# One-hots and spread positions of a graph layer built by two-tensor compares

## The reference

```python
x_j = x[src]
x_i = x[dst]
msg = concatenate([x_i, x_j - x_i], axis=-1)
h = relu(msg @ W1 + b1)
h = relu(h @ W2 + b2)
h = relu(h @ W3 + b3)
m = h @ W4 + b4
s = segment_sum(m, dst, 12500)
cnt = segment_sum(ones, dst, 12500)
out = layernorm(x + s / maximum(cnt, 1)[:, None])
```

## Time and profile before

| | us |
|---|---|
| median of 3 runs | 1553.71 (1542.68 to 1553.79) |
| the profiled execution | 1556.37 |
| its span, first to last instruction | 1554.5 |
| busy: matrix engine, weight loads | 1375.3, 930.6 |
| busy: Vector engine, ScalarE, GpSimd | 966.0, 605.6, 1168.6 |

### The profile page before, as it was taken

The page is one execution under the profiler, slowest core; times in us unless marked ns, Lnnn a source line. Parts: engine busy times, 40 slices in busy tenths (PEclk is TensorE's granted clock), DMA queues, the critical chain, the costliest instruction groups (busy, mean ns, idle before and its releaser), DMA issues.

```text
span 1554.5 us, 40899 instructions
## 1 busy us (share of the span) xinstructions
PE 1375.3 (88%) x14064; PEld 930.6 (60%) x14064; DVE 966.0 (62%) x3159; ACT 605.6 (39%) x952; POOL 1168.6 (75%) x1101
## 2 busy tenths in 40 slices
PE   3254999999999999999989999999899989999676
PEld 2112666666767766766756666666566656766443
DVE  5986566666666666666556666665556655666355
ACT  5354333443343443444333433434324343333323
POOL 4777777777777777777777777777777777777752
PEclk8566999999999999999999999999989998999868
DMA  7538977777767777777667777767657775775411
GB/s 183 163 88 188 296 232 228 220 223 225 226 202 233 232 225 220 224 214 228 185 176 224 209 225 215 213 201 203 196 173 233 209 217 171 233 221 158 105 30 44
DMA packets 197031, 306.55 MB, mean 197 GB/s; under 512 B 84519, under 2 KB 90010, under 8 KB 196257
## 3 DMA queue, kind: packets, MB, share of 16 engines
q1 hardware_dynamic: 161485, 267.17, 56.2%
q0 software_dynamic: 34656, 34.90, 10.5%
q10 hardware_dynamic: 682, 1.85, 0.5%
HBM read 289.68 MB, written 13.92 MB: 195 GB/s over the span
## 4 chain that ended last, share of the span: by engine, by line
POOL 66%; issue 20%; DVE 5%; PE 3%; DMA 3%; SPq 2%; ACT 0%; DVEq 0%; POOLq 0%; ACTq 0%
POOL xj L585 66%; DVE region L1290 1%; DVE region L1291 1%; DMA sums<-in_src 1%; SPq L524 1%; DMA x_rows<-x_p 1%; PE ps L964 1%; DMA xj<-z_rows,src_t 1%; DVE work L1156 0%; PE ps L1019 0%; PE ps L988 0%; DVE work L1162 0%; PE ps L996 0%; DMA region<-src_rows 0%; PE ps L1081 0%
## 5 line engine op out<-in xcount | busy, mean ns | idle before, releaser
L585 POOL DMA_INDIRECT xj<-z_rows,src_t x1043 | 1111.1, 1065 | 317.9 <-issue 317.0
L964 PEld LDWEIGHTS ps<-region,x_p 128*96 128x96 bf16 x6780 | 397.8, 126 | 53.8 <-issue 53.2
L964 PE MATMUL ps<-region,x_p 128*96 128x127 bf16 (+54 forms) x6780 | 418.6, 220 | 8.1 <-DVE region L1380 8.1
L731 ACT ACTIVATE work<-ps,b3s 128x512 f32<-128x512 f32 x196 | 134.7, 687 | 562.7 <-PE ps L996 554.7
L1380 DVE TENSOR_SCALAR region<-region,cst 128x1629 bf16<-128x1629 int16 x480 | 302.1, 630 | 13.3 <-DMA region<-src_rows 13.1
L1395 DVE COPY work<-ps 128x512 f32<-128x512 f32 x195 | 133.9, 687 | 271.2 <-PE ps L1004 268.9
L724 ACT ACTIVATE work<-ps,b2s 128x512 f32<-128x512 f32 x392 | 248.0, 683 | 69.8 <-PE ps L988 69.8
L716 ACT ACTIVATE work<-ps,b1s 128x512 f32<-128x512 f32 x196 | 134.7, 687 | 237.8 <-PE ps L901 237.5
L988 PE MATMUL ps<-work,w2s 64*128 64x512 f32 x784 | 224.9, 651 | 1.0 <-ACT work L716 0.9
L996 PE MATMUL ps<-work,w3s 128*64 128x512 f32 x784 | 213.3, 623 | 0.0
L1410 DVE TENSOR_SCALAR region<-iota_g,dst_rel 128x42 f32<-128x42 f32 x1056 | 206.7, 251 | 0.0
(11 more groups left out here) (156 smaller groups left out, 810.1 us busy)
## 6 DMA issues: line engine op xcount, KB each, us to landing
dstb<-dst_rows SPq DMA_DIRECT2D x196, 252.0 KB
region<-src_rows SPq DMA_DIRECT2D x120, 391.2 KB
region<-src_rows SPq DMA_DIRECT2D x60, 407.2 KB
region<-src_rows SPq DMA_DIRECT2D x60, 403.2 KB
region<-src_rows SPq DMA_DIRECT2D x60, 376.2 KB
region<-src_rows SPq DMA_DIRECT2D x60, 375.8 KB
region<-src_rows SPq DMA_DIRECT2D x60, 374.0 KB
region<-src_rows SPq DMA_DIRECT2D x60, 366.2 KB
```

The lines of the kernel that those rows point to most:

```text
L585: pool.indirect_dma_start(out=xj[:, u, j % UT, j // UT, 0:w], out_offset=None, in_=rows, in_offset=bass.IndirectOffsetOnAxis(ap=cols[:, j: ...
L731: nc.scalar.activation(h3[:, v, :], p_h3, ACT.Relu, bias=b3s[:, 0:1]).then_inc(s_r3, 1)
L964: chosen = nc.tensor.matmul(ps[0:XP, XBANK[h], lo - h * UE:hi - h * UE], xb[:, a, :], hot[:, q % QN, at + lo:at + hi], start=not begun[h], ...
```

## The change

The chunks' compare takes the partition's number as a second tensor that repeats the column, in place of a scalar operand. The one-hots of a step are built by two instructions of four tiles each, comparing a repeated row of node numbers with repeated columns of targets, in place of eight instructions of one tile. The order in a step is rewritten for this: one-hots, a chunk, one-hots, a chunk, sums, a chunk; in the step ahead of a sorted one the wide pick stands in the first chunk's place, and the two chunks follow behind the one-hots and behind the sums.

```diff
                     if b and c == piece[0]:
                         dve.wait_ge(s_block, len(PIECES) * (b - 1) + i + 1)
-                nc.vector.tensor_scalar(hot[:, q % QN, 0:CW[c]], spread[:, q % QE, 0:CW[c]], cst[:, C_PID:C_PID + 1], None,
-                                        ALU.is_equal).then_inc(s_hot, 1)
+                nc.vector.tensor_tensor(hot[:, q % QN, 0:CW[c]], spread[:, q % QE, 0:CW[c]],
+                                        cst[:, C_PID:C_PID + 1].to_broadcast([P, CW[c]]), ALU.is_equal).then_inc(s_hot, 1)
...
-            def build_onehot(s, tiles):
+            def build_onehot(s, j0, j1):
                 v, n = s % 2, STEPS[s]
                 nodes, w = (iota_s, WIN) if n < SB else (iota_g, KN)
-                for j in tiles:
-                    last = nc.vector.tensor_scalar(onehot[:, v, j, 0:w], nodes[:, :],
-                                                   dst_rel[:, n * PT + j:n * PT + j + 1], None, ALU.is_equal)
-                if j == PT - 1:
-                    last.then_inc(s_oh, 1)
+                made = nc.vector.tensor_tensor(onehot[:, v, j0:j1, 0:w],
+                                               nodes[:, :].unsqueeze(1).to_broadcast([P, j1 - j0, w]),
+                                               dst_rel[:, n * PT + j0:n * PT + j1].unsqueeze(2).to_broadcast([P, j1 - j0, w]),
+                                               ALU.is_equal)
+                if j1 == PT:
+                    made.then_inc(s_oh, 1)
...
                     build_pick(s + 1)
                 if s <= S_N + 2:
                     onehot_free(s - 3)
-                    build_onehot(s - 3, (0, 1))
+                    build_onehot(s - 3, 0, PT // 2)
                 if s + 1 < S_N and is_sorted(s + 1):
                     build_wide_pick(s + 1)
+                else:
+                    hot_of(s, 0)
                 if s <= S_N + 2:
-                    build_onehot(s - 3, (2, 3))
-                hot_of(s, 0)
-                if s <= S_N + 2:
-                    build_onehot(s - 3, (4, 5))
-                hot_of(s, 1)
-                if s <= S_N + 2:
-                    build_onehot(s - 3, (6, 7))
+                    build_onehot(s - 3, PT // 2, PT)
+                if s + 1 < S_N and is_sorted(s + 1):
+                    hot_of(s, 0)
+                else:
+                    hot_of(s, 1)
                 add_sums(s - 4)
-                hot_of(s, 2)
+                if s + 1 < S_N and is_sorted(s + 1):
+                    hot_of(s, 1)
+                else:
+                    hot_of(s, 2)
```

## The result

The changed kernel takes 2027.32 us (2026.29 to 2032.86, 4 runs) beside 1553.75 us for the kernel before: a ratio of 1.308, 95% interval 1.301 to 1.314. Slower was forecast, at 1930 us, with a range of 1690 to 2070; the measured time lies inside it, near its upper end. The profiled execution has a span of 2024.7 us, 470.2 more than before.

The account below looks back on a forecast made before the run. GpSimd's gathers were taken as the bound: 986 x 1.245 + 480 x 0.98 + 31 = 1729 us where 1349 stood, +380; with -2 behind the last gather this gave 1930 us, range 1690 to 2070.

Parts of the forecast that it names:

- The bound: GpSimd's gathers at L585, 66% of the chain before, were to stay the bound after the change.
- The prices of the instructions: On the Vector engine: a hot 1.76 us, 168 columns of one-hots 0.32, and L1418's 0.497 for 336 columns.
- The mechanism: A gather beginning inside a compare or an instruction with both inputs in SBUF stands until that instruction's end.
- the third rival: A hot with one repeated column runs as with a scalar, 0.63 us; about 16 us gained; chance 0.03.
- 480 x 0.98 = 470: Gathers in the main loop: 480 hots keep them waiting 0.98 us each, 470 us in all.
- the forecast's 31 us for all else: Gathers held by one-hot halves (7 and 8 us) and by picks (16 us), 31 us in the main loop.
- each catches one, and only one: A hot of 1.76 us, longer than the gathers' spacing of 1.245, holds exactly one gather.
- the second rival: No gather is let in between a hot, the one-hot behind it and the next hot: +160, 2090; chance 0.12.
- The one-hots' term: Merged one-hots hold gathers 7 us (264 halves) and 8 us (120 halves), where the old ones in pairs held 31.
- The cover: The Vector engine's spare 5 us per period hides its new order, priced at nothing; 22.9 us against the gathers' 28.2.

Follow-up runs that it names:

- pair of runs with a reduction and a compare of the same length: The kernel before with an unused 1080-column instruction behind every hot: 1696.84 us with a one-input reduction, 1902.98 us with a two-input compare.
- with gaps: The changed kernel with the Vector engine waiting for its own instruction's end behind each hot and each half of the one-hots: 1956.77 us, ratio 1.260.
- the run with one-hots alone: The changed kernel, with merged one-hots and new order, but with the old one-input compare for the hots: 1571.04 us, ratio 1.011.

## Why the prediction was right, and what in it was off

**The bound** was right: the gathers were most of the chain before (66%) and are after (80%), and the span rose by their stretch to 3 us.

**The prices of the instructions** were right: hots 1.76 us (1.756 measured), one-hots 0.32 us (0.322), and the 0.497 of L1418 for the wide halves (0.498). The estimate from the Trainium skill (VectorE: DVE Perf Modes, on the TRN2 errata), 1.67 us, was too low by 0.09, as the row of L1418 had said.

**The mechanism** was right: a gather that begins inside such an instruction stands to its end, and the repeated column holds it as L1129 did. The pair of runs with a reduction and a compare of the same length shows it by itself: a stretch of 138 us against 470, and gathers of 0.945 us against 1.84 beside the added instruction. What the Trainium skill says of the two SBUF inputs (GPSIMD Engine Reference, Key points) agrees with these two pairs of numbers; the third rival, in which the column costs nothing, fell.

**The term that was mis-sized** is "480 x 0.98 = 470". Less the forecast's 31 us for all else, the measured stretch leaves 564, or 1.17 us per hot. The step behind it was "each catches one, and only one". Gather by gather, over the loop: in the changed kernel 362 gathers stood behind one hot each, 0.92 us in the mean, near the forecast's 0.98; but 57 stood through two or three hots, 242 us in all. That was the second rival, priced at +160 us with a chance of 0.12. It happens in part, 49 times of the 57 where the 1629-column hot, 336 columns of one-hots and the 1496-column hot follow one another, and it is worth some 75: with gaps 480 gathers stood behind one hot each, 0.99 us in the mean, and none behind two; the stretch falls to 520, and (520 - 31) / 480 = 1.02 us per hot. Of the 94 us that the term lacked, these gathers are 75, and the other 19 lie in the size per hot. The rival's picture was incomplete too: 28 of the 57 had already been caught by the pick ahead and stood 4.6 us each, not 3.0.

**The one-hots' term** had the wrong sign. Their short holds were to cost 15 us in place of 31. Alone, the merging and the new order cost 14 us of span, and on top of the changed hots 77 (2024.7 less 1947.3). In the run with one-hots alone the holds of one hot or none did get cheaper, by 29 us; the 32 more gathers that stood through two or three hots cost 47. That one long instruction between two hots closes a place at which gathers were let in fits this, but the merging and the new order were not run apart.

**The cover** held: the Vector engine's own work is 0% of the chain of the changed kernel. At which time it would have become the bound there, no run shows. The run with the reduction, in which the Vector engine is busy 138 us longer and in the old order, was bound by it at 1697 us.

## What to carry to other kernels

When GpSimd's indirect DMAs are the path, an instruction of another engine is to be priced by what it keeps waiting, not by its own busy time: here each hot that held them for longer than their spacing was stood through once, by a gather of its own or by one that stood through two, and the same compare in two halves cost about half. Look in the timelines for the transfer's shortest time and for what runs beside each one that took longer. Then cut the long holds, or give the engine that has time to spare a wait for its own end behind each, and measure: here such waits brought the kernel before 1.1%, and the one with merged one-hots and the old hots 3 to 4% against the kernel before. Waits behind the hots alone made the kernel before 0.9% slower.

## What the runs showed of the hardware that was not expected

A gap of some 0.03 us between two instructions of the Vector engine, made by a wait for its own semaphore, was enough to let a waiting gather in: at the end of the 1629-column hot 51 of 51 where 2 of 51 had been let in. It was not enough everywhere: with waits behind the hots alone, none of 22 at the end of the 1613-column ones. Without such a wait it depends on the place: in the changed kernel 57 of 59 were let in between a hot of 1565 columns and 168 columns of one-hots, with no wait between them. What makes the two places differ is open; width, buffer and step differ together, and no run here parts them.

A reduction of 1080 float columns out of SBUF, 1.263 us long, added 16 us to the stretch over 480 of them, and no gather whose wait could begin inside one took more than 1.02 us; a compare with a second input of the same length added 348.

Merging eight instructions into two, in the new order, made the kernel slower by 1.1%, and adding waits to it then made it faster than before by 3 to 4%.
